# Layer normalization of a transformer layer's input: five of sixteen row tiles moved to GpSimd

## The reference

```python
x = L0_attn_hidden_states            # (1, 2048, 256)
xn = (x - mean(x)) / sqrt(var(x) + 1e-05)        # over the last axis
x = x + attention(xn, Wq, bq, Wk, bk, Wv, bv, Wo, bo) + experts(xn, router_w, gate_w, up_w, down_w)
```

## Time and profile before

| | us |
|---|---|
| median of 3 runs | 376.69 (376.27 to 377.09) |
| the profiled execution | 375.99 |
| its span | 374.2 |
| PE busy in the span | 365.2 (98%) |
| DVE busy | 327.7 (88%) |
| ACT busy | 269.1 (72%) |
| POOL busy | 72.3 (19%) |

### The profile page before, as it was taken

How to read it: one execution, slowest core, us unless ns; L and a number is a source line. 1 busy time by engine, 2 the same in 40 slices (tenths; PEclk the granted TensorE clock), 3 DMA queues, 4 the chain that set the end, 5 groups by cost and what they waited for, 6 DMA issues and landing times.

```text
span 374.2 us, 12333 instructions
## 1 busy us (share of the span) xinstructions
PE 365.2 (98%) x4702; PEld 204.3 (55%) x4702; DVE 327.7 (88%) x675; ACT 269.1 (72%) x546; POOL 72.3 (19%) x87
## 2 busy tenths in 40 slices
PE   8899899999999999999999999999999999999996
PEld 3655466766665564555545546455464554643365
DVE  5877889997768999999999999999999999998656
ACT  4736567564446888888888888888888888899920
POOL 3024824542000022020220202122122020210002
PEclk9999999999999999999999999999999999999999
DMA  7997856756310212222132221322313222111116
GB/s 231 297 372 290 261 164 215 218 163 168 110 54 30 59 33 61 63 75 74 35 84 70 58 68 39 91 77 58 88 32 93 62 56 76 32 39 39 25 35 228
DMA packets 32027, 40.46 MB, mean 108 GB/s; under 512 B 11108, under 2 KB 26468, under 8 KB 31520
## 3 DMA queue, kind: packets, MB, share of 16 engines
q1 hardware_dynamic: 29768, 34.42, 30.8%
q0 software_dynamic: 1872, 5.11, 5.0%
q10 hardware_dynamic: 336, 0.20, 0.3%
HBM read 25.65 MB, written 11.70 MB: 100 GB/s over the span
## 4 chain that ended last, share of the span: by engine, by line
PE 87%; DVE 4%; DMA 3%; ACT 2%; issue 2%; POOL 1%; SPq 0%; ACTq 0%; POOLq 0%; DVEq 0%
PE ps L822 22%; PE ps L852 21%; PE ps L747 14%; PE ps L698 6%; PE ps L760 6%; PE ps L711 5%; PE ps L830 3%; PE ps L736 2%; DMA o_st<-sorted_rows,token_of 2%; DMA x_sb<-x_in 2%; PE ps L612 1%; PE ps L723 1%; PE ps L601 1%; PE ps L684 1%; POOL o_st L513 1%
## 5 line engine op out<-in xcount | busy, mean ns | idle before, releaser
L1157 DVE TENSOR_REDUCE mx<-ps 128x1 f32<-128x512 f32 x232 | 150.7, 685 | 3.2 <-PE ps L747 0.7
L1487 ACT ACTIVATE probs<-ps 128x512 f32<-128x512 f32 x192 | 102.0, 598 | 19.0 <-PE ps L852 18.0
L852 PE MATMUL ps<-q_op,k_op 98*32 98x512 bf16 (+1 forms) x1104 | 112.1, 381 | 0.1
L747 PE MATMUL ps<-k_op,q_op 96*32 96x512 bf16 x672 | 76.1, 381 | 0.0
L1160 DVE TENSOR_REDUCE mx_tail<-ps 128x2 f32<-128x410 f32 x116 | 66.8, 576 | 3.4 <-PE ps L760 3.2
L852 PEld LDWEIGHTS ps<-q_op,k_op 98*32 98x32 bf16 (+1 forms) x1104 | 39.6, 96 | 33.0 <-issue 6.1
L822 PE MATMUL ps<-probs,v_op 128*32 128x512 f32 x384 | 52.4, 592 | 0.0
L519 POOL COPY v_op<-v_all 128x192 f32<-128x192 f32 x16 | 6.9, 437 | 188.3 <-PE ps L822 188.2
L1487 ACT ACTIVATE dn<-ps 77x512 f32<-77x512 f32 x64 | 34.3, 592 | 8.2 <-PE ps L852 8.2
L747 PEld LDWEIGHTS ps<-k_op,q_op 96*32 96x32 bf16 x672 | 25.0, 95 | 22.4 <-DVE mx L1157 8.0
L1487 ACT ACTIVATE gu<-ps 128x512 f32<-128x512 f32 x64 | 33.2, 604 | 4.9 <-PE ps L852 4.9
(11 more groups left out here) (148 smaller groups left out, 500.0 us busy)
## 6 DMA issues: line engine op xcount, KB each, us to landing
q_parts<-parts SPq DMA_DIRECT2D x12, 256.0 KB
sorted_results<-ys SPq DMA_DIRECT2D x23, 128.0 KB
gu<-gu_in SPq DMA_DIRECT2D x1, 2816.0 KB, 15.1
q_op<-q_parts SPq DMA_DIRECT2D x11, 192.0 KB, 3.2
sorted_rows<-xn SPq DMA_DIRECT2D x4, 512.0 KB, 11.7
xnT<-o_st SPq DMA_DIRECT2D x62, 32.0 KB, 2.0
tab<-softmax_recips SPq DMA_DIRECT2D x15, 128.0 KB
x_sb<-x_in SPq DMA_DIRECT2D x3, 512.0 KB, 6.8
```

The source lines that it names most:

```text
L747: ins = pe.matmul(bank(t % 2)[r:r + CW, :], q_op[slot][0:KR, P * t + r:P * t + r + CW], k_op[slot][0:KR, 0:NWIDE], start=True, stop=True)
L852: ins = pe.matmul(bank(4 + u % RING)[r:r + w, :], k_op[h % OPS][:, c0 + r:c0 + r + w], q_op[h % OPS][:, QB * b:QB * b + QB], start=True, s ...
L1157: dve.tensor_reduce(mx[:, slot, t:t + 1], bank(t % 2)[:, 0:NWIDE], AX.X, ALU.max).then_inc(wide_reduced, 1)
L1487: act.activation(prob[c][0:rows, QB * b:QB * b + QB], bank(4 + u % RING)[0:rows, :], ACT.Exp, scale=SCALE).then_inc(exp_done, 1)
```

## The change

Five tiles are normalized on GpSimd, by the same instruction as on DVE: 5 and 7 of group 1, 9 and 11 of group 2, 15 of group 3. DVE keeps tiles 0, 1, 4, 8, 12, 13 and ACT 2, 3, 6, 10, 14. GpSimd waits for `scale_ready` of each group, and a new semaphore `xn_on_pool` tells PE and SP of its tiles. On DVE, the statistics of tile 8 move ahead of `normalize(1)`. On ACT, root 2 moves ahead of the copy of pair 3, and normalize 2 ahead of the first projection's bias.

```diff
+NORM_DVE = ((0, 1), (4,), (8,), (12, 13))
+NORM_ACT = ((2, 3), (6,), (10,), (14,))
+NORM_POOL = ((), (5, 7), (9, 11), (15,))
...
+        def on_pool(tile):
+            return sum(t < tile for group in NORM_POOL for t in group)
...
             for g in range(4):
                 sp.wait_ge(xn_ready, g + 1)
                 sp.wait_ge(xn_on_act, g + 1)
+                if g:
+                    sp.wait_ge(xn_on_pool, on_pool(4 * g + 4))
                 sp.dma_start(nv[:, 4 * g:4 * g + 4, :], xn[:, 4 * g:4 * g + 4, :]).then_inc(xn_stored, 16)
...
             pool.wait_ge(iota_ready, 3)
+            for g in range(1, 4):
+                pool.wait_ge(scale_ready, g + 1)
+                for t in NORM_POOL[g]:
+                    pool.tensor_scalar(xn[:, t, :], x_sb[:, t, :], mv[:, t, 0:1], rstd[:, t:t + 1],
+                                       ALU.subtract, ALU.mult).then_inc(xn_on_pool, 1)
             pool.wait_ge(logits_T_ready, 1)
...
                 else:
                     pe.wait_ge(xn_on_act, pair // 2 + 1)
+                if on_pool(2 * pair + 2) > on_pool(2 * pair):
+                    pe.wait_ge(xn_on_pool, on_pool(2 * pair + 2))
...
-                for t in range(4 * g, 4 * g + 2):
+                for t in NORM_DVE[g]:
                     ins = dve.tensor_scalar(xn[:, t, :], x_sb[:, t, :], mv[:, t, 0:1], rstd[:, t:t + 1],
...
             moments(1)
+            statistics(8, 9)
             normalize(1)
-            statistics(8, 12)
+            statistics(9, 12)
...
-                for t in range(4 * g + 2, 4 * g + 4):
+                for t in NORM_ACT[g]:
                     ins = act.activation(xn[:, t, :], x_sb[:, t, :], ACT.Identity, bias=shift[:, t:t + 1],
...
             copy_xT(2)
+            root(2)
             copy_xT(3)
-            root(2)
+            normalize(2)
             act.wait_ge(bqk_in, 16)
             biased(0, 0)
-            normalize(2)
             copy_xT(4)
```

More of the change, by code:

```diff
@@ L75 @@
 OPS = RING + 1
+NORM_DVE = ((0, 1), (4,), (8,), (12, 13))
+NORM_ACT = ((2, 3), (6,), (10,), (14,))
+NORM_POOL = ((), (5, 7), (9, 11), (15,))
+assert sorted(sum(NORM_DVE + NORM_ACT + NORM_POOL, ())) == list(range(NT))
 ROUNDS = (HEADS - 4) // RING
@@ L222, in layer @@
         var_ready, std_ready, xn_ready = sem("var_ready"), sem("std_ready"), sem("xn_ready")
-        scale_ready, xn_on_act = sem("scale_ready"), sem("xn_on_act")
+        scale_ready, xn_on_act, xn_on_pool = sem("scale_ready"), sem("xn_on_act"), sem("xn_on_pool")
         last_xnT_ready = sem("last_xnT_ready")
```

## The result

| | before | changed |
|---|---|---|
| median of 13 runs | 376.69 us | 379.97 us |
| ratio to before | | 1.0079 (95% interval 1.0059 to 1.0099) |
| profiled execution, its span | 375.99, 374.2 us | 380.58, 378.5 us |

What follows compares the result with a forecast made beforehand. PE, with 87% of the 374.2 us span, was taken to bound the kernel and carry shifts to the end one for one. A front gain of 0.11 from 376.69 gave 376.58, say 376.6 us; range 375.9 to 377.9.

Steps and rivals of the forecast that it cites:

- the price of GpSimd's tile: Normalizing one 128x256 tile on GpSimd, priced from rows of other operations: 0.40 us taken.
- The upper end, 0.74: Highest price taken for one GpSimd tile, from the add of two tensors; it put the kernel at 377.1 us.
- Rival 1: GpSimd's tile is slow, so pair 3 waits for tile 7: at 1.1 us a tile +1.16, 377.85 us; chance 0.17.
- Its formula for the wait: Front shift at pair 3 is about 2T - 1.04 us, T being GpSimd's time for one tile, once T is over 0.6.
- "Hidden" for tile 15: Group 3: GpSimd's tile 15 ready at 16.7 to 17.1 us, wanted by PE at about 17.6, so no cost.
- "Hidden" for tiles 9 and 11: Group 2: ready at about 13.7 and 14.1 us (14.0 and 14.8 if slower), wanted at 14.32 and 14.9; no cost.
- The transfer to the end: From the front PE carries any shift to the end one for one; a gain at 44.67 is capped at 0.36 us.
- rival 4: Gathers on GpSimd meet DVE's work otherwise; one more long one costs 0.8 us, giving 377.5; chance 0.09.
- The lock (rival 2): DVE's normalization locks GpSimd out, which begins only behind tile 4: +0.22 to +0.77 us, 376.9 to 377.5; chance 0.12.
- Rival 3: Transfers gain: SP's earlier store brings expert load and tables forward, at most 1.26 idle us, 375.4; chance 0.12.
- the forecast's own sum 0.90 us: GpSimd time for one tile from which the slow-tile case decides, the front then being 0.76 us late.

Runs made afterwards that it cites:

- e1_fill: The changed kernel with nine more filler products on PE before pair 2 and two between pairs 2 and 3; 378.95 us, ratio 1.0042.
- e2_group1_back: The changed kernel with tiles 5 and 7 back on DVE and ACT, GpSimd keeping 9, 11 and 15; 379.09 us, ratio 1.0042.
- e3_idle: The kernel before with the six filler products ahead of pair 2 taken out; 377.96 us, ratio 1.0016.
- e4_order_only: The changed kernel with no tile on GpSimd, only the new order on DVE and ACT; 377.27 us, ratio 1.0009.
- e6_tile15_back: The changed kernel with tile 15 back on ACT, GpSimd keeping 5, 7, 9 and 11; 379.30 us, ratio 1.0069.
- e12_one_tile: The changed kernel with only tiles 7 and 11 on GpSimd, DVE two tiles a group, ACT 6, 10, 14 and 15; 376.65 us, ratio 1.0001.
- e9_less_fill: e4_order_only without the two pairs of filler products around the first projection; ratio 1.0012.
- e10_table_first: The kernel before with the load of the second table part issued ahead of the big expert load; ratio 0.9985.
- e11_both: e9_less_fill with the table load of e10_table_first; 376.28 us, ratio 0.9979.
- e7_shift: The kernel before with 20 filler products in place of 6 ahead of pair 2; 377.79 us, ratio 1.0026.
- e8_dve_quiet: The changed kernel with DVE held, except its own two group 3 tiles, until GpSimd's tile 15 is done; tile 15 took 1.48 us (one execution).

## Why the prediction was wrong, point by point

Delays in us, from the start of the statistics of group 1 on, against the kernel before:

| kernel | token list | turn behind the fourth gather | clock falls in its trace | ratio |
|---|---|---|---|---|
| changed | 3.79 | 3.25 | yes | 1.0079 |
| e1_fill | 2.15 | 2.41 | no | 1.0042 |
| e2_group1_back | 1.23 | 0.91 | no | 1.0042 |
| e3_idle | 1.47 | 2.28 | yes | 1.0016 |
| e4_order_only | -0.20 | -0.27 | no | 1.0009 |
| e6_tile15_back | 2.43 | 2.18 | yes | 1.0069 |
| e12_one_tile | 0.92 | 1.38 | no | 1.0001 |
| e9_less_fill | -0.37 | 0.51 | no | 1.0012 |
| e10_table_first | -0.02 | -0.53 | no | 0.9985 |
| e11_both | 0.42 | -1.06 | yes | 0.9979 |

(e7_shift is left out: there PE's own work and not the statistics sets the front. The one trace of e11_both has a late load of group 1, PE idle 3.01 us and a fall of the clock; what its turn gains all the same is not taken apart.)

- **The step that failed is the price of GpSimd's tile**: "I take 0.40, the middle of the copy's two, since the tile reads one tensor as the copy does". It is 1.22. The number of tensors read does not set it: with one tensor and one multiplication per partition GpSimd takes 0.918, more than the add of two tensors (0.744). The second operation adds 0.30, and numbers per partition in place of constants 0.14 of the whole; why one operation costs 0.918 where a copy costs 0.34 to 0.46 stays open. The upper end, 0.74, was the row of a cheaper form, so it was no bound. The Trainium skill, "GPSIMD Engine Reference" (Engine selection), calls one-input work there roughly line-rate; here GpSimd takes 1.217 us for the tile that DVE normalizes in 0.407, and the measurement decides.
- **Rival 1 was the case**, with 0.17. Its formula for the wait holds: 2 x 1.22 - 1.04 = 1.40, and pair 3 came 5.35 - 3.83 = 1.52 us late (3.83 is 11.50 - 7.67 of before); the rest is mostly PE's start, 0.15 behind the end of tile 7 (13.68 - 13.53) where the forecast had 0.04. Its time does not hold: even with T = 1.22 it would have been 376.69 + 1.40 = 378.1, and 380.0 was measured. The rest is the next two points.
- **"Hidden" for tile 15 failed by the same price.** It ended 1.81 + 0.10 behind the shift, and PE waited 0.63 us. "Hidden" for tiles 9 and 11 held only because PE was late: e2_group1_back shows their waits.
- **The clock was missing altogether.** I asked what PE's wait costs in time and not what PE's idleness costs afterwards. At the token list that is 1.64 us (changed kernel less e1_fill), as much as the wait itself, and e3_idle has 1.47 without any wait moved. Read along the changed kernel's own trace, pair 3 is 1.52 late, pair 4 is 3.05 late (9.70 against 14.32 - 7.67 = 6.65), pair 7 waits 0.63 more, and with 0.11 of smaller pieces the token list is 3.79 late. (1.52 + 1.64 + 0.63 is 3.79 too, but 1.64 is itself a difference of two such delays; the step from pair 3 to pair 4 is 1.53.) At the turn behind the gather only 0.84 of the 1.64 is left, so what the fall costs at the end is known only roughly.
- **The transfer to the end held roughly.** The idle time of 0.90 at 41 us did absorb (no PE idle from 40 to 45 us in the changed kernel), and the gather then set the turn. Its delay fell from 3.79 to 3.25 since the fourth gather landed 6.15 us behind its start, where it took 6.96 before; it started 5.29 behind the first, where it was 5.05. At the end 3.0 are left. That the gathers vary was rival 4, and it worked the other way here.
- **The lock (rival 2)** I had set aside since DVE's 0.407 showed no doubled rate. GpSimd is held up all the same (e8_dve_quiet, e12_one_tile), by 0.17 to 0.27 us a tile beside two tiles of DVE and by 0.6 with the product and the comparison as well, but it is not kept from starting. In groups 1 and 2 of the changed kernel, with one tile on DVE, it cost 0.02 and 0.10, so it isn't the cause.
- **Rival 3** could not come true by GpSimd: SP's fourth store had to wait for tile 15, and the expert load behind it was issued at 22.26 in place of 18.88. Moved by hand (e10_table_first), the table load does take PE's idle 1.26 us away, and puts a wait of 0.89 us in front.

What stays open: the times of e2_group1_back and e1_fill are alike (1.0042) though their token lists are 0.9 us apart. A trace is one execution: that of e2_group1_back is the fastest of its 12 (377.84 beside a median of 379.09), that of e1_fill is above its median (379.80 beside 378.95). So the delays of the table are good for saying where time goes within an execution, and no ratio follows from one of them.

## What to carry to other kernels

An operation priced from other rows of an engine needs a row of its own form: neither the number of inputs nor that of arithmetic steps gave the price here. Where there is no such row, the upper end is a guess, and it should be asked instead how slow the operation may be before it hurts (by the forecast's own sum 0.90 us). Where TensorE has filler work to keep its clock, a late operand can cost twice, once as the wait and once as the clock behind it, so it is worth asking how long the fillers last if the operand is late; fillers are not free either (e7_shift, 14 more, 1.0 us with an interval of 0 to 2.0). One tile a group on GpSimd, the last of its group, cost nothing that could be measured (to 0.24%) though PE waited 0.37 us for the first of them; two in a row, with tile 15, cost 0.8%.

## What the runs showed of the hardware that I had not expected

- GpSimd's tensor_scalar on 128x256 float32 with two operations and numbers per partition: 1.217 us alone, 0.786 for 128 columns, 1.075 with constants, 0.918 with one operation.
- DVE's float32 tensor_scalar with numbers per partition holds GpSimd's up: 1.39 to 1.48 us in place of 1.22, with 0.45 to 0.55 us in which both run, though its own 0.407 for 256 columns is that of the one-source statistics, which hold nothing up (1.21).
- TensorE's granted clock fell to half between 11 and 18 us in five of the profiled executions, for about 3.4 us each. PE had been idle in the front just before: 2.18 and 0.59 us (changed kernel), 1.97 (e6_tile15_back), 1.56 and 0.59 (e8_dve_quiet), 3.01 (e3_idle and e11_both). In e10_table_first 1.67 us of idle time left it at 1.00. Runs of the kernel before with a mean clock of 0.996 or less are 1.6 to 2.1 us longer than those with 0.999 or more (378.27 against 376.69, 378.88 against 376.77); this holds also what made PE wait in them. They are 10 of 35, 2 of 17 and 6 of 35 runs.
